# LSTM stage: one written order for a whole turn on VectorE and ScalarE, TensorE's order left as it was

## The reference, cut to what matters

```
h = relu(layernorm(x))
h = relu(adj @ (h @ Wg0 + bg0));  h = relu(adj @ (h @ Wg1 + bg1))
for p in 1..4:                       # in order, each on the h that the one before left
    windows = h cut along the nodes into 128 // p windows of p nodes
    h_last  = LSTM_p(windows)        # p steps, start state zero, gates i, f, g, o
    h[last node of each window] = h_last
x = x + h
```

## Time and profile before

| | |
|---|---|
| median of three runs | 1310.18 us |
| profiled execution, its span | 1309.45 us, 1307.6 us |
| busy: TensorE, weight loads, VectorE, ScalarE, GpSimd | 91%, 78%, 77%, 62%, 32% of the span |
| LSTM stage | from 37 us to 737 us of the span |
| one turn | 86.7 us |
| granted TensorE clock | 0.979 on average; 1.00 in the LSTM stage after its first turn |

### The profile page before, as it was taken

One profiled execution on the slowest core, in us unless ns is written; L12 is line 12 of the kernel. 1 busy time (PEld: TensorE's weight loads), 2 busy tenths in 40 slices (PEclk: granted clock), 3 DMA queues, 4 the chain that ended last, 5 costly groups with the idle time before them and its releaser, 6 DMA issues. The chain is left out here.

```text
span 1307.6 us, 24530 instructions
## 1 busy us (share of the span) xinstructions
PE 1192.5 (91%) x7808; PEld 1024.9 (78%) x7808; DVE 1010.0 (77%) x2796; ACT 812.9 (62%) x1804; POOL 412.6 (32%) x779
## 2 busy tenths in 40 slices
PE   2889999899899998998999799998999899968998
PEld 1678788787787886877878688886777688857997
DVE  6677877878778778777787699997777578775776
ACT  3477575775765757757667576776777376742332
POOL 3110200200102002001020277775767488832332
PEclk7899999999999999999999899999999899988999
DMA  9300000000000000000000000000000000001222
GB/s 269 93 1 1 1 1 1 0 0 0 0 0 0 0 0 0 0 0 0 0 1 1 1 2 2 2 2 1 1 1 1 1 1 2 2 1 40 72 72 72
DMA packets 24728, 21.09 MB, mean 16 GB/s; under 512 B 1744, under 2 KB 20304, under 8 KB 24400
## 3 DMA queue, kind: packets, MB, share of 16 engines
q1 hardware_dynamic: 24656, 20.21, 5.4%
HBM read 11.82 MB, written 8.39 MB: 15 GB/s over the span
## 5 line engine op out<-in xcount | busy, mean ns | idle before, releaser
L557 ACT ACTIVATE gate<-ps,b_lstm 128x256 f32<-128x256 f32 (+2 forms) x624 | 300.4, 558 | 36.8 <-PE ps L584 36.8
L582 PE MATMUL ps<-H_hi,w_hi 128*128 128x256 f32 (+2 forms) x624 | 212.4, 342 | 42.1 <-ACT gate L557 25.3
L583 PE MATMUL ps<-H_hi,w_lo 128*128 128x256 f32 (+2 forms) x624 | 205.3, 330 | 0.0
L584 PE MATMUL ps<-H_lo,w_hi 128*128 128x256 f32 (+2 forms) x624 | 195.9, 335 | 6.6 <-DVE H_lo L526 5.2
L126 POOL TENSOR_SCALAR rstd<-mv 128x8 f32<-128x8 f32 x18 | 12.3, 685 | 600.5 <-DVE mv L107 600.4
L582 PEld LDWEIGHTS ps<-H_hi,w_hi 128*128 128x128 f32 x624 | 117.5, 188 | 68.2 <-ACT gate L557 32.6
L567 ACT ACTIVATE tanh_c<-cell 128x512 f32<-128x512 f32 (+2 forms) x176 | 90.4, 514 | 127.6 <-DVE cell L517 81.7
L584 PEld LDWEIGHTS ps<-H_lo,w_hi 128*128 128x128 f32 x624 | 114.6, 189 | 25.1 <-DVE H_lo L526 17.5
L583 PEld LDWEIGHTS ps<-H_hi,w_lo 128*128 128x128 f32 x624 | 117.8, 189 | 7.6
L582 PE MATMUL ps<-hid_hi,w_hi 128*128 128x256 f32 (+2 forms) x384 | 119.0, 316 | 0.8 <-DVE hid_hi L523 0.8
L583 PE MATMUL ps<-hid_hi,w_lo 128*128 128x256 f32 (+2 forms) x384 | 117.3, 312 | 0.0
(11 more groups left out here) (206 smaller groups left out, 3102.8 us busy)
## 6 DMA issues: line engine op xcount, KB each, us to landing
out<-x SPq DMA_DIRECT2D x32, 256.0 KB, 2.3
w_raw<-in_WihT SPq DMA_DIRECT2D x1, 1024.0 KB, 8.6
w_raw<-in_WhhT SPq DMA_DIRECT2D x1, 1024.0 KB, 8.1
wqkvT<-in_WqkvT SPq DMA_DIRECT2D x1, 192.0 KB, 4.9
w_sb<-in_W SPq DMA_DIRECT2D x1, 192.0 KB, 4.6
ends_row<-in_src_row SPq DMA_DIRECT2D x1, 128.0 KB, 3.6
ends_row<-in_dst_row SPq DMA_DIRECT2D x1, 128.0 KB, 3.7
x<-in_x_in SPq DMA_DIRECT2D x8, 0.5 KB, 10.5
```

The costliest lines, as they stand in the source:

```text
L557: nc.scalar.activation(gate[:, g, z, 0:w * GB], gate_bank(g, k, m)[:, 0:w * GB], ACT.Tanh if z == G else ACT.Sigmoid, bias=b_lstm[:, 4 * ( ...
L582: nc.tensor.matmul(dst, w_hi[:, src, p - 1, z], v_hi, start=start, stop=False)
L583: return nc.tensor.matmul(dst, w_lo[:, src, p - 1, z], v_hi, start=False, stop=False)
L584: return nc.tensor.matmul(dst, w_hi[:, src, p - 1, z], v_lo, start=False, stop=stop)
```

## The change

Each engine's turn is now one string of letters. a and b stand for the next part of group 0 and of group 1, s and t for the next piece of norming of group 0 and 1; a capital stands for a part of the turn before. `merged` walks the string. TensorE's string spells the same sequence of instructions as before, all 146 parts of a turn. VectorE's and ScalarE's strings give another order. The arithmetic, the shapes and the number of instructions stay; STATS and APPLY are issued one by one. Three waits are added on ScalarE: gates I and G of k = 1 wait for the cell of k = 0; the first APPLY of a group waits also for A0 of the same turn on TensorE.

```diff
-        STATS_AT = {U1: (0, 3), A1: (3, 3), STEP: (6, 2)}
-        AGGR_AT = STEP + 1
-        APPLY_AT = {STEP + 3: (0, 1), STEP + 4: (1, 2), STEP + 5: (3, 2), STEP + 6: (5, 1), STEP + 8: (6, 1),
-                    STEP + 9: (7, 1)}
-        def interleave(engine, parts):
...
+        for k in range(NS):
+            n = len(gates_of[k])
+            TENSOR_PARTS += [(SHARE, k, m) for m in range(n) if recurrent(k)] + [(HIGH, k, 0), (LOW, k, 0)]
+            TENSOR_PARTS += [(REST, k, m) for m in range(2, n)]
+            VECTOR_PARTS += [(KEEP, k, 0)] * recurrent(k) + [(CELL, k, 0), (HIDDEN, k, 0)] + [(LOW, k, 0)] * (k < NS - 1)
+            SCALAR_PARTS += [(GATE, k, m) for m in range(n)] + [(TANH, k, 0)]
+        MOMENTS = [(STATS, j, 0) for j in range(GB)] + [(AGGR, 0, 0)]
+        NORMED = [(APPLY, j, 0) for j in range(GB)]
+        ON_VECTOR = ("stttsttaBaBBsatasbssbssaabbaabbsababaaaabbabbaatbbaabaabbaabbabbaaaabtbtbaabbaabbaabbabbaaaabbba"
+                     "aabbabbaabbbba")
+        ON_SCALAR = ("BBaaBBBbbaaaaababsaaaabbbbaaabbabbaaaabbabbsaaaabbbbbaaaabsbabbaaabbbaasbbttaaaabbbbtbttaaasaabb"
+                     "bbaaabaabbbtssbaaasbbbbbaatt")
+        def merged(engine, order, do, main, side):
+            parts = {"a": main, "b": main, "s": side, "t": side}
+            late = {z: order.count(z.upper()) for z in parts}
+            def turn(i, first, last):
+                taken = {z: len(parts[z]) - late[z] for z in parts}
+                for letter in order:
+                    z = letter.lower()
+                    part = parts[z][taken[z] % len(parts[z])]
+                    taken[z] += 1
+                    g = int(z in "bt")
+                    if last and i == TURNS:
...
+                    elif letter == z:
+                        do(i, g, *part, not first)
+                    elif not first:
+                        do(i - 1, g, *part, True)
...
+                        if apart[k] and z == O:
+                            act.wait_ge(sa(g, "a_h32"), i * (NS - 1) + k)
+                        elif apart[k]:
+                            act.wait_ge(sa(g, "a_cell"), i * NS + k)
...
+                    elif what == APPLY:
+                        if k == 0:
+                            act.wait_ge(sa(g, "a_shift"), i + 2)
+                            act.wait_ge(sa(g, "a_axp"), i * CH + CH)
+                        relu_norm(act, i + 1, g, k, 1)
```

More of the change, by code:

```diff
@@ L326, in _ @@
                 for g in range(2):
+                    act.wait_ge(sa(g, "a_shift"), 1)
                     relu_norm(act, 0, g, 0, GB)
@@ L392, in four_layers @@
         TG, TP = gates_before[NS], parts_before[NS]
-        A0, OUT, W0, U1, A1, STEP = range(6)
-        ITEMS = STEP + NS
-        STATS_AT = {U1: (0, 3), A1: (3, 3), STEP: (6, 2)}
-        AGGR_AT = STEP + 1
-        APPLY_AT = {STEP + 3: (0, 1), STEP + 4: (1, 2), STEP + 5: (3, 2), STEP + 6: (5, 1), STEP + 8: (6, 1),
-                    STEP + 9: (7, 1)}
-        def interleave(engine, parts):
-            def turn(i, first, last):
[L407 to L412, removed]
+        A0, OUT, W0, U1, A1, SHARE, HIGH, LOW, REST, GATE, KEEP, CELL, TANH, HIDDEN, STATS, AGGR, APPLY = range(17)
@@ new lines, in recurrent @@
+        def recurrent(k):
+            return steps[k][1] > 0
+        by_chunk = lambda *what: [(q, c, 0) for q in what for c in range(CH)]
+        TENSOR_PARTS = by_chunk(A0, OUT, W0, U1, A1)
+        VECTOR_PARTS = by_chunk(OUT, W0, U1, A1)
+        SCALAR_PARTS = by_chunk(A0, A1)
+        for k in range(NS):
[4 more added lines that the diff above has]
+            SCALAR_PARTS += [(GATE, k, m) for m in range(n)] + [(TANH, k, 0)]
@@ L416, in interleave @@
                 turn(i, False, False)
[L417 to L423, removed]
+            turn(TURNS - 1, False, False)
+            turn(TURNS, False, True)
         def gate_bank(g, k, m):
@@ L456, in _, with turn @@
             def _(pool):
-                def item(i, g, n, more, _):
-                    if n == AGGR_AT:
+                def turn(i):
+                    for g in range(2):
                         make_rstd(pool, i + 1, g)
-                interleave(pool, [(item, 0, 0), (item, 1, 1)])
+                turn(0)
+                with pool.Fori(1, TURNS - 1) as i:
+                    turn(i)
+                turn(TURNS - 1)
             @block.vector
             def _(dve):
[L465 to L472, removed]
-                        norm_aggr(g * GB, GB, sa(g, "a_aggr"))
@@ L475, in item @@
[L475 to L504, removed]
@@ L527, in item @@
                                 sa(g, "a_lo"), 1)
-                        else:
-                            nc.vector.tensor_tensor(h32, go, tc, ALU.mult).then_inc(sa(g, "a_hid"), 1)
-                interleave(dve, [(item, 0, 0), (item, 1, 1)])
+                merged(dve, ON_VECTOR, part, VECTOR_PARTS, MOMENTS)
             @block.scalar
             def _(act):
[L535 to L547, removed]
@@ L549, in gates @@
-                def gates(i, g, n, *_):
-                    k = n - STEP
-                    if k >= 0:
-                        p, j, last, w0, w = steps[k]
[L553 to L559, removed]
-                                                     sa(g, "a_gate"), 1)
@@ L584, in term @@
                     return nc.tensor.matmul(dst, w_hi[:, src, p - 1, z], v_lo, start=False, stop=stop)
-                def input_share(i, g, n, *_):
-                    k = n - STEP
-                    if k >= 0 and steps[k][1] > 0:
-                        p, j, _, w0, w = steps[k]
-                        for m, z in enumerate(gates_of[k]):
-                            pe.wait_ge(sa(g, "a_gate"), i * TG + gates_before[k] + m - 3)
-                            for part in (0, 1):
-                                term(g, k, m, z, 0, at(H_hi[:, g], p, j, w0, w), at(H_lo[:, g], p, j, w0, w),
-                                     True, False, part)
@@ L625, in item, with part @@
-                def item(i, g, n, more, before):
-                    if n == A0:
+                def part(i, g, what, k, m, before):
+                    if what == A0:
                         if before:
                             pe.wait_ge(sa(g, "a_gate"), i * TG)
-                        for c in range(CH):
-                            pe.wait_ge(sa(g, "a_hn"), i * GB + (c + 1) * CB)
-                            for b in range(CB):
-                                ins = nc.tensor.matmul(ps[:, 4 * g + c, b * T:(b + 1) * T],
-                                                       hn[:, g * GB + c * CB + b], adjT_sb[:], start=True, stop=True)
-                            ins.then_inc(sa(g, "a_axp"), 1)
-                    elif n == OUT:
+                        pe.wait_ge(sa(g, "a_hn"), i * GB + (k + 1) * CB)
+                        for b in range(CB):
+                            ins = nc.tensor.matmul(ps[:, 4 * g + k, b * T:(b + 1) * T],
+                                                   hn[:, g * GB + k * CB + b], adjT_sb[:], start=True, stop=True)
+                        ins.then_inc(sa(g, "a_axp"), 1)
+                    elif what == OUT:
@@ L670, in four_layers @@
+                merged(pe, ON_TENSOR, part, TENSOR_PARTS, [])
         part0.close()
```

194 lines of the change are left out of this document (121 added, 73 removed).

## The result

The changed kernel takes 1279.84 us (median, 1278.75 to 1280.79); beside it the kernel before took 1311.33 us. The ratio is 0.976, with a 95% interval of 0.9743 to 0.9777: 31 us less. The forecast was 1262 us with a range of 1246 to 1285 us. The sign is right and the time lies in the range, but of the 48 us that the sum gave only two thirds came.

The account below looks back on a forecast made before the run. TensorE was taken as the bound, waiting 9.7 us of an 86.7 us turn. Turns of 80.5 us, 49.6 us over eight, less 1.2 and 0.4, gave 48 us: 1262 us for the median, range 1246 to 1285 us.

Parts of the forecast that it names:

- The bound and the ceiling: LSTM turn of 86.7 us: TensorE's own work 77.0, waits 9.7; at most 78 us to gain, floor 1231 us.
- The gate waits: TensorE's three waits for ScalarE to read a gate's bank, 4.1 us a turn, go; new wait at 1:SHARE6O, 0.8 to 0.9.
- A1: Group 1's A1, low part awaited at 1:HIGH0: the wait falls from 1.6 to 0.5 us a turn.
- HIGH and LOW waits: TensorE's waits for a new h's high and low parts: 4.0 us in 7 places falls to 2.7 us a turn.
- AGGR: VectorE, group 0: moving it ahead of CELL0 is free and gives 0.6 us back between CELL1 and HIDDEN1.
- Turn's start: STATS at VectorE's head, 0:OUT ahead of 1:KEEP10: costs nothing while 0.5 us of slack holds, else at most 1.3 us a turn.
- rival A: Only TensorE's gate waits go, HIGH and LOW waits stay: 32 us gained, 1278 us; chance 0.19.
- B: Rival: nearly all of TensorE's waits go, 1.5 to 2 us a turn stay: 66 us gained, 1243 us; chance 0.11.
- C: Rival: TensorE's waits only move, VectorE's or ScalarE's capacity being the bound: no change, 1309 us; chance 0.06.
- D: Rival, convoys: one group's part held behind the other's in six places, +3.2 us a turn, 1335 us; chance 0.06.
- E, the lock: Rival: CELL0 on VectorE held to the end of GpSimd's 1.95 us, +1.9 us a turn, 1277 us; chance 0.03.
- The end of the stage: Last turn: 1:KEEP10 behind 0:OUT makes the LSTM stage end 1.2 us later, once.

Follow-up runs that it names:

- tenth kernel: Kernel with both G10O gates moved ahead: 0:AGGR back between 0:CELL1 and HIDDEN1, 0:APPLY0 back behind 0:TANH3; 1265.2 us, ratio 0.9649.
- ninth kernel: Kernel with both G10O gates moved ahead (1266.4 us): on VectorE 1:KEEP10 goes ahead of the first 0:OUT at the turn's start; 1264.9 us, ratio 0.9654.
- first two experiments: Each against the changed kernel, ScalarE only: 0:G10O ahead of 1:TANH9, 1274.0 us; 1:G10F and G10O ahead of 0:A0's copies, 1273.5 us.
- best kernel measured: Both G10O gates moved ahead on ScalarE, and 1:KEEP10 ahead of the first 0:OUT on VectorE; 1264.9 us, ratio 0.9654.
- either half alone: Changed kernel with one engine's order put back: ScalarE's new order over VectorE's old steps, 1322.7 us; VectorE's new order with ScalarE's old, 1323.1 us.

## Why the prediction was right and where it was wrong

**The bound and the ceiling: right.** TensorE's own work was put at 77.0 us a turn. After, 82.9 us less the 6.6 us of waits listed is 76.3. Counted alike, with the wait of 0.3 us for `hid_lo`, the kernel before has 86.7 - 10.0 = 76.7 us. So the waits fell by 3.4 us of the 3.8 us that a turn gained, and W0's wait for 0:OUT, 0.2 us, went too. The last 0.2 us may be what TensorE loses in restarts; no run separates it.

**The gate waits: right.** All three went, and 1:SHARE6's fourth gate came with 0.9 us, as said.

**A1 and the HIGH and LOW waits: right in size.** A1 leaves 0.7 us against 0.5 predicted. High and low parts leave 0.7 + 1.2 + 1.0 = 2.9 us against 2.7. The weight loads' timeline names the places:

| | 0:HIGH2 | 0:LOW2 | 1:LOW4 | 1:LOW7 | 0:LOW5 | 0:LOW8 | 1:LOW3 |
|---|---|---|---|---|---|---|---|
| predicted | 0.5 | 0.5 | 0.5 | 0.3 | 0.4 | 0.5 | - |
| measured | 0.68 | 0.56 | 0.46 | 0.20 | 0.23 | 0.45 | 0.30 |

Six of the seven were named. The list of those that go held one that was never there (1:HIGH6) and one that the 4.0 us did not count (1:LOW6, the wait for `hid_lo` before). The reasons given for single ones were partly off. AGGR gave nothing (the tenth kernel), and the trace of the kernel before could have told it: 0:HIDDEN1 starts 0.69 us after the end of 0:CELL1, with AGGR in between, no later than the 0.70 us that TANH alone keeps VectorE waiting. VectorE's idle time for TANH fell from 9.6 to 6.4 us, not to 3; it is idle time of an engine that is not the bound.

**Turn's start: the step that failed.** "The cost is nothing while that half microsecond holds." For what it followed (OUT, KEEP10, HIDDEN10, W0) this is true, as the ninth kernel shows. But it asked what waits for VectorE and left out what waits for ScalarE. A0 waits on `a_gate`, a wait that in the kernel before was never late and so had no row. But it was close. ScalarE's four gates 1:G10 there, and 1:A0 on TensorE:

```profile
211.68 1.57 ACT L557 ACTIVATE gate<-ps,b_lstm 128x256 f32<-128x256 f32 x4
```

```profile
213.30 2.05 PE L632 MATMUL ps<-adjT_sb,hn 128*128 128x128 f32 x16
```

The last gate ends 0.05 us ahead of 1:A0; for 0:A0 the room was 0.5 us. Both moves that take this room are in the change: 0:G10O goes behind 1:TANH9, as spelled out ahead of the prediction, and the copies of 0:A0, which stood ahead of all four 1:G10 gates, go between 1:G10G and G10F, as ScalarE's string has it. Neither was priced. They cost 2 x 1.0 us a turn by the first two experiments, and 13 us less is measured with both gates moved ahead, of the 18 us between forecast and result. The sum would have been 80.5 + 2.1 = 82.6 us a turn, against 82.9 measured. The rest, 0.3 us a turn or some 3 us, may be A1's 0.2 and the parts' 0.2; no run takes it apart. That the time lies in the range all the same is luck in part: the sum is 18 us off, and the range reaches up to 1285 us to take in rival A, not because a term of the sum could be so large.

**The rivals.** The result stands at rival A's 1278 us, by accident: A has the gate waits as the only gain and the HIGH and LOW waits unchanged. In fact the gate waits gave 3.2 us a turn, A1 0.9 and the HIGH and LOW waits 1.4 (4.3 with `hid_lo` to 2.9), and A0 took 2.1 back. B is not reached by the best kernel measured (1265 us). C is refuted by the turns. D's mechanism shows in either half alone, at 1.7 and 1.3 us a turn against the 3.2 that D gave it; in the combined order the two crossings at LOW cost 0.7 us of waits and bring more. E, the lock, does not show: 0:CELL0 takes 0.69 us beside GpSimd's pow instruction (1.67 us from 220.81):

```profile
221.48 0.69 DVE L533 TENSOR_TENSOR cell<-gate 128x512 f32<-128x512 f32 x1 [1.19 <-ACT gate L573]
```

**The end of the stage.** KEEP10 stands behind 0:OUT, as said. Against the 1.2 us for it the ninth kernel's trace shows 0.9; the times can't confirm it.

## What to carry to other kernels

When an order is changed on some engines only, list every semaphore that the unchanged engine waits on, those first that were never late: a wait without a row in the trace of before is still there, with some slack, and the trace tells how much: here 0.05 and 0.5 us. The two cost 13 us of a gain that would have been 43. Judge a merged order for several engines as one object, since each half alone was slower than no change. Before removing a wait that a crossing makes, ask what it fills: undoing the ones at LOW cost 4 us. And an earlier arrival gains nothing where the next wait is for the same chain, as at 0:HIGH2.

## What the runs showed of the hardware

GpSimd's small instructions took longer beside a run of VectorE's instructions on two SBUF inputs, while VectorE's were slowed by at most 0.05 us. Before, group 0's L126 took 0.74 us and L128 1.95 us; in the changed kernel, with only 0:CELL0 beside them, 0.24 and 1.67. With AGGR put back (tenth kernel) both return. GpSimd and then VectorE in that kernel:

```profile
222.53 0.74 POOL L126 TENSOR_SCALAR rstd<-mv 128x8 f32<-128x8 f32 x1 [46.45 <-DVE mv L107]
223.35 1.95 POOL L128 TENSOR_TENSOR rstd<-rstd,half 128x8 f32<-128x8 f32 x1
```

```profile
222.48 0.69 DVE L541 TENSOR_TENSOR H_hi<-gate,tanh_c 128x512 fp32r<-128x512 f32 x1
223.09 0.68 DVE L542 TENSOR_TENSOR H<-gate,tanh_c 128x512 f32<-128x512 f32 x1
223.81 0.69 DVE L548 TENSOR_TENSOR H_lo<-H,H_hi 128x512 fp32r<-128x512 f32 x1
```

L126 starts 0.05 us after HIDDEN1 and ends 0.1 us after it, 0.5 us longer than alone. The Trainium skill's rule (SBUF — State Buffer, section "Who interferes with whom") has whoever comes second held to the other's end; the trace agrees where GpSimd comes second. It does not where VectorE does: `H_lo` starts within the 1.95 us and takes 0.69. The longest that VectorE's instruction of this size took there is 0.74 us, at 225.80, where it starts 0.01 us after GpSimd's L134 of 0.21 us. GpSimd's spans are rough, so the sizes of its own times are less sure than VectorE's.
